# Feed-forward weights quantised and transposed inside the first group of time mixing, instead of in a stage of their own

## The chip, the cores and the metric

The kernel runs on one core of a Trainium2 chip. TensorE (PE), VectorE (DVE), ScalarE (ACT), GpSimd (POOL) and SyncE (SP) run side by side and wait for each other through semaphores. SyncE issues all the transfers of this program. The metric is the device time of one execution in microseconds; the time before is 2716.16 us, the median of three runs (2716.14 to 2721.93).

## The reference

One layer in three parts, each with a layer norm ahead and a residual behind: cross attention, time mixing (a recurrent state over 32 tokens) and a feed-forward with ternary weights. x is (128, 32, 256). The parts that the change touches:

```
x = x + xattn(layernorm(x), ctx)
x = x + time_mixing(layernorm(x))
x = x + ffn(layernorm(x))

def act_quant(x):                       # 8 bits per token
    scale = 127.0 / clip(max(abs(x), -1), EPS)
    return clip(round(x * scale), -128, 127) / scale

def weight_quant(w):                    # ternary
    scale = clip(mean(abs(w)), EPS)
    return clip(round(w / scale), -1, 1) * scale

def h_bitlinear(x, w):                  # fwht: Hadamard transform
    return act_quant(fwht(x)) @ weight_quant(w).T

gate, up = h_bitlinear(x, w_gate), h_bitlinear(x, w_up)     # (1024, 256) each
return h_bitlinear(silu(gate) * up, w_down)                 # (256, 1024)
```

## The kernel before

Cross attention runs first and ends at about 2010 us of the span. It leaves its result in DRAM. After a barrier `time_mixing` (line 1129) runs, then `feed_forward` (line 1688). Both are written out by hand: each engine has a list of its own, and semaphores join the lists.

**Time mixing** has the 128 sequences on the partitions and takes the 32 tokens in eight groups of T = 4. `run(step)` calls `step(j, j % 2)` for j = 0 to 9 on each engine. In step j, group j is mixed and projected, group j-1 goes through the recurrence (`scan_out`, `scan_in`, on VectorE with the state in PSUM), and group j-2 is normalised, gated, projected and stored. Group j+1 is transposed (`columns`, `shift`) and group j+2 normalised.

What group 0 goes through, in order:

- SyncE (lines 1213 to 1238): `load(0)` and `load(1)` bring two groups of rows; then fourteen loads of weights and small vectors, then 32 loads of eight values each (`gw` and `gb`, sixteen times each, lines 1224 to 1226), all on `w_loaded`; then `load(2)`, `load(3)`, and per group `load(j + 4)` and `store(j)`. A load of group j waits until group j-2 is normalised. `store(j)` loads the residual's rows into `xr`, waits for the result and stores `x2`.
- ScalarE (lines 1454 to 1462): sums, squares and normalisation of groups 0 and 1, the transposed columns of group 0, the tanh of `low_rank(0)`.
- VectorE (lines 1585 to 1594): waits for all of `w_loaded`, centres `wv` (two instructions, `vmean` and `wv`), then `shift(0)`: the difference `dT` and the first mixture `xp`.
- TensorE: `columns(0)`, waits for `w_loaded` and `wv_ready`, `low_rank(0)` (line 1260), then in `step` the mixes 0 to 3, `decay`, mixes 4 and 5, the transposes of group j-2, mixes 6 to 9 (each a product of 32 rows by 512 columns, line 1271), and the projections `project(j, 0..3)`, `low_rank(j + 1)` and `gates(j)`.
- Each mix goes from TensorE to VectorE (`mix`, line 1482) and to GpSimd (`xm`, line 1621). `decay` waits for the first two `xm`, `project(j, 0)` for the first eight.
- GpSimd also makes the layer norm's roots, the outer products `kv` and the column of the current token in `prod` (`own_values`, line 1640).

The tiles `x2`, `oT`, `o`, `sgT`, `osq` and `prod` are first written in the later steps: `prod` at `own_values(0)`, `sgT[0]` at `gates(0)`, `o[0]` and `osq` in step 1, `oT` and `x2` in step 2.

**The feed-forward** begins with a block of its own (lines 1707 to 1788): three weights of 1 MB are loaded, with the Hadamard matrix behind them. VectorE takes the absolute sum of each (line 1740), makes the scaled copies of the Hadamard matrix (lines 1744 and 1746), takes the scales from a product with a matrix of ones, and makes each weight ternary in three passes (lines 1757, 1759 and 1761: scale and min, max and add MAGIC, subtract MAGIC into bf16). TensorE transposes each in 16 pieces (line 1779) and ScalarE copies them to `wgT`, `wuT` and `wdT` (line 1788). The block ends with a barrier. Then the second block works through 32 tiles of 128 tokens (one per position), pipelined over six steps: it loads the rows `x`, transposes them (line 1868), copies them to `hT` (line 1966), rotates them with `had_x` (line 1898), quantises, and so on.

## Time and profile before

| what | value |
|---|---|
| median of three runs | 2716.16 us |
| lowest, highest | 2716.14, 2721.93 us |
| the profiled execution's own time | 2719.26 us |
| its span | 2717.5 us |
| mean granted TensorE clock | 0.939 |
| PE busy | 2492.1 us (92%) |
| DVE busy | 1983.9 us (73%) |
| ACT busy | 1666.3 us (61%) |
| POOL busy | 1203.6 us (44%) |

The page and the tables are of one execution, recorded by the hardware profiler. All positions in time are microseconds from the start of its span. A timeline row gives the start, the duration, the engine, the line, the operation, what it writes and reads, its shape and how many instructions are merged in the row; in brackets stands how long the engine was idle before, and what ended the wait. SPq rows are issues of transfers, not the transfers. The granted clock is a share of full speed: 1.00 is 2.4 GHz and 0.50 is 1.2 GHz.

### The profile page before, as it was taken

To read this page: it belongs to the slowest core of one execution; us is meant where nothing else is said; L and a number is where in the kernel's file an instruction comes from. 1 tells how busy PE (TensorE), PEld (TensorE's weight loads), DVE (VectorE), ACT (ScalarE), POOL (GpSimd) and SP (SyncE) were. 2 spreads that over 40 slices of the span, in tenths; PEclk is the share of its full clock that TensorE was granted. 3 is DMA by queue.
4 is the path that set the end of the run, shared out by engine and by line. 5 is a ranking of instruction groups with operands and counts; after the bars stand their busy time and mean duration, and the time that the engine had idled before them with its cause. 6 is when DMAs were issued, how large, how long until landed. Compare 5 with 4: busy or idle time off the path is not lost. (4 is left out here: it accounts for less than half of the span.)

```text
span 2717.5 us, 51029 instructions
## 1 busy us (share of the span) xinstructions
PE 2492.1 (92%) x14035; PEld 2025.8 (75%) x14035; DVE 1983.9 (73%) x4330; ACT 1666.3 (61%) x3281; POOL 1203.6 (44%) x1935
## 2 busy tenths in 40 slices
PE   8999999999979967999999999999959999838998
PEld 6777777777758857998989899899944454426886
DVE  7999999999956635776767676667734787867886
ACT  6777777777745535666666566666644444316776
POOL 2210111100137733655555555555626676606775
PEclk9999999999989988999999999999987787859999
DMA  3000000000012214344344333444420010021111
GB/s 120 24 26 26 26 26 26 26 26 26 20 45 67 66 30 153 114 115 112 113 118 118 112 117 110 114 113 116 116 87 16 24 47 16 32 71 43 53 52 39
DMA packets 234985, 183.49 MB, mean 68 GB/s; under 512 B 37169, under 2 KB 226834, under 8 KB 234258
## 3 DMA queue, kind: packets, MB, share of 16 engines
q1 hardware_dynamic: 234770, 180.90, 23.0%
q8 instruction: 101, 1.65, 0.3%
q14 instruction: 114, 0.93, 0.1%
HBM read 152.74 MB, written 28.06 MB: 67 GB/s over the span
## 5 line engine op out<-in xcount | busy, mean ns | idle before, releaser
L255 DVE TENSOR_REDUCE kn_ssq<-kn_sq 128x8 f32<-128x1024 f32 x514 | 621.2, 1215 | 72.4 <-ACT kn_sq L197 67.0
L197 ACT ACTIVATE kn_sq<-kn_keys 128x1024 f32<-128x1024 f32 x514 | 528.0, 1027 | 178.5 <-PE kn_keys L146 176.2
L146 PE MATMUL kn_keys<-kn_wk_hi,kn_ct_hi 128*128 128x512 f32 x1028 | 334.1, 406 | 0.9 <-ACT kn_sq L197 0.9
L146 PE MATMUL kn_keys<-kn_wk_lo,kn_ct_hi 128*128 128x512 f32 x1028 | 320.9, 393 | 0.0
L146 PE MATMUL kn_keys<-kn_wk_hi,kn_ct_lo 128*128 128x512 f32 x1028 | 320.4, 393 | 0.0
L1012 DVE CUSTOM_DVE_ANT_0 ca_sc<-ca_b_sc,ca_rk,ca_rq_rows 128x257 f32<-128x257 f32 x512 | 230.7, 482 | 82.2 <-issue 81.9
L967 ACT ACTIVATE ca_sc<-ca_sc,ca_low 128x257 f32<-128x257 f32 x512 | 254.4, 499 | 12.5 <-DVE ca_low L1045 4.8
L1115 POOL TENSOR_TENSOR ca_sc<-ca_sc,ca_rden 128x1028 f32<-128x1028 f32 x128 | 243.3, 1901 | 10.0
L146 PEld LDWEIGHTS kn_keys<-kn_wk_lo,kn_ct_hi 128*128 128x128 f32 x1028 | 193.3, 188 | 45.0
L146 PEld LDWEIGHTS kn_keys<-kn_wk_hi,kn_ct_lo 128*128 128x128 f32 x1028 | 193.3, 188 | 44.4
L146 PEld LDWEIGHTS kn_keys<-kn_wk_hi,kn_ct_hi 128*128 128x128 f32 x1028 | 165.3, 189 | 69.4 <-ACT kn_sq L197 55.9
L1113 POOL TENSOR_TENSOR ca_pl<-ca_sc,ca_rden 128x4 f32<-128x4 f32 x128 | 25.5, 199 | 418.0 <-DVE ca_rden L1067 418.0
L954 ACT ACTIVATE ca_pT_hi<-ca_b_p 128x512 fp32r<-128x512 f32 x256 | 139.7, 595 | 96.4 <-PE ca_b_p L869 96.4
L818 PE MATMUL ca_b_sc<-ca_cT_hi,ca_u_hi 128*128 128x258 f32 x512 | 161.5, 315 | 29.5 <-issue 10.6
L33 POOL TENSOR_TENSOR kn_mark<-kn_ident 1x1 f32<-1x1 f32 x66 | 12.1, 183 | 368.4 <-DVE kn_ssq L255 365.6
L1022 DVE TENSOR_TENSOR ca_oT_lo<-ca_b_val,ca_oT_hi 128x512 fp32r<-128x512 f32 x128 | 88.5, 692 | 110.7 <-ACT ca_oT_hi L974 110.7
L1050 DVE TENSOR_TENSOR ca_pT_lo<-ca_b_p,ca_pT_hi 128x512 fp32r<-128x512 f32 x256 | 164.9, 686 | 0.1
L818 PE MATMUL ca_b_out<-vo_hi,ca_oT_hi 128*128 128x256 f32 x512 | 155.4, 303 | 1.8 <-DVE ca_x L1035 1.8
L820 PE MATMUL ca_b_sc<-ca_cT_hi,ca_u_lo 128*128 128x258 f32 x512 | 147.5, 288 | 0.0
L819 PE MATMUL ca_b_sc<-ca_cT_lo,ca_u_hi 128*128 128x258 f32 x512 | 147.3, 288 | 0.0
L869 PE MATMUL ca_b_p<-ca_ident,ca_sc 128*128 128x128 f32 x1024 | 136.5, 276 | 9.4 <-issue 9.4
L819 PE MATMUL ca_b_out<-vo_lo,ca_oT_hi 128*128 128x256 f32 x512 | 144.4, 282 | 0.0
(316 smaller groups left out, 6770.9 us busy)
## 6 DMA issues: line engine op xcount, KB each, us to landing
ca_rk<-key_norms SPq DMA_DIRECT2D x512, 128.5 KB, 2.9
kn_rows<-in_ctx_dram SPq DMA_DIRECT2D x128, 128.0 KB, 2.4
ca_rows<-in_ctx_dram SPq DMA_DIRECT2D x128, 128.0 KB, 2.7
ca_xT<-normed_columns SPq DMA_DIRECT2D x16, 512.0 KB, 4.6
ca_vs_rows<-last_values SPq DMA_DIRECT2D x96, 64.0 KB, 2.6
qn_x<-in_x_dram SPq DMA_DIRECT2D x32, 128.0 KB, 2.5
normed_columns<-qn_xT_hi SPq DMA_DIRECT2D x32, 128.0 KB, 1.8
normed_columns<-qn_xT_lo SPq DMA_DIRECT2D x32, 128.0 KB, 1.8
```

The lines of the kernel that those rows point to most:

```text
L146: mm = pe.matmul(keys[c][:, n * 512:(n + 1) * 512], a, w[:, c * CH + n * 512:c * CH + (n + 1) * 512], start=first, stop=last)
L197: act.activation(sq[c][:, :], keys[c][:, :], ACT.Square).then_inc(sq_ready, 1)
L255: dve.tensor_reduce(ssq[s][:, t * H + c * (H // 2):t * H + (c + 1) * (H // 2)], sq[c][:, :].rearrange("p (h d) -> p h d", d=P), AX.X, ALU. ...
L818: pe.matmul(out, a_hi, w_hi, start=first, stop=False)
L819: pe.matmul(out, a_hi, w_lo, start=False, stop=False)
L820: return pe.matmul(out, a_lo, w_hi, start=False, stop=final)
L869: mm = pe.transpose(b_p[k][:, g * P:(g + 1) * P], s[:, g, k * P:(k + 1) * P], ident[:, :])
L954: act.activation(pT_hi[:, k, :], b_p[k][:, :], ACT.Copy).then_inc(phi_ready, 1)
L967: act.activation(sc[bb % 4][:, g, :], sc[bb % 4][:, g, :], ACT.Exp, bias=low[n][:, g:g + 1], scale=1.0, accum_out=den[n][:, g:g + 1]).then ...
L1012: dve.tensor_tensor_reduce(sc[bb % 4][:, g, :], b_sc[g % 2][:, 0:SKV], rk[n][:, g, :], rq_rows[i][:, bb % PER // 4, g, bb % 4:bb % 4 + 1], ...
L1050: dve.tensor_tensor(pT_lo[:, k, :], b_p[k][:, :], pT_hi[:, k, :].bitcast(F32), ALU.subtract).then_inc(plo_ready, 1)
L1115: pool.tensor_tensor(probs[:, :, :], probs[:, :, :], rden[m][:, :].unsqueeze(2).broadcast_to((P, 4, SKV)), ALU.mult)\
```

## The change

- The transposed weights (`ff_cols`) and their scales (`ff_scale`) are allocated outside both functions. `time_mixing` fills them and `feed_forward` gets them.
- The whole first block of `feed_forward` is gone, with its barrier. Its Hadamard load stands behind the first tile's load. Its scaled copies stand on VectorE between the statistics of tile 0 and of tile 1, and the rotation of tile 0 waits for them. The identity and the constants are made at the start of the remaining block.
- In `time_mixing` the raw weights are loaded in six halves of 512 KB, behind `wx1`, `wv`, `mu` and `load(1)` and ahead of the other weights. They lie in tiles that group 0 doesn't need yet (`x2`, `oT`, `o[1]`, `sgT[1]`, `osq`), and the ternary values in `prod`.
- VectorE takes six absolute sums ahead of its wait for `w_loaded`. The scales and the passes of weight 0 come after `shift(0)`, those of weight 1 after mix 3 of group 0, those of weight 2 after its mix 9. Each pass is two instructions of 1024 columns.
- TensorE transposes weight 0 between mix 3 and `decay(0)`, weight 1 between mix 5 and mix 6, weight 2 between `project(0, 1)` and `project(0, 2)`. ScalarE copies them out after `decay(0)`, after the squares of group 2, and after the last `take`. They use the PSUM banks `b_o`.
- The first uses of the borrowed tiles get waits: `scan_out` and `own_values` for the last transposes, `gates` and SyncE's first two row loads for the last ternary values.
- The 32 small loads stand behind `load(3)` on a semaphore of their own, `affine_loaded`, for which ScalarE waits at its first affine step.
- The residual's rows are loaded into `x2` itself. The load waits for the store of two groups before; `xr` is gone.

Time mixing's side, cut to its core:

```diff
+        raw = [w.rearrange("p a b -> p (a b)") for w in (x2[0][:, :, :], x2[1][:, :, :], oT[:, :, :], o[1][:, :, :], sgT[1][:, :, :])] + [osq[:, :]]
+        tern = [prod[n // 2][:, :, :, :].rearrange("p h v k -> p (h v k)").bitcast(BF16)[:, (n % 2) * F:(n % 2 + 1) * F] for n in range(6)]
...
-        WEIGHTS = 14 + 2 * (P // HV)
+        WEIGHTS = 14
...
             load(0)
+            sp.dma_start(wx1[:, :, :], wx1_dram.rearrange("(a p) n -> p a n", p=P)).then_inc(w_loaded, 16)
+            sp.dma_start(wv[:, :, :], wv_dram.rearrange("(a p) n -> p a n", p=P)).then_inc(w_loaded, 16)
+            for a in range(2):
+                sp.dma_start(mu[:, a:a + 1], mu_dram[a * P:(a + 1) * P].rearrange("(p a) -> p a", a=1)).then_inc(w_loaded, 16)
             load(1)
...
+            for n in range(2):
+                for h in range(2):
+                    sp.dma_start(raw[2 * n + h].rearrange("p (r n) -> p r n", r=4),
+                                 ff_dram[n].rearrange("(h r p) n -> h p r n", h=2, p=P)[h]).then_inc(raw_loaded[n], 16)
+            for h in range(2):
+                sp.dma_start(raw[4 + h], ff_dram[2][h * P:(h + 1) * P, :]).then_inc(raw_loaded[2], 16)
+            for w, d in ((wr, wr_dram), (wk, wk_dram), (wg, wg_dram), (ww1, ww1_dram), (wo, wo_dram)):
                 sp.dma_start(w[:, :, :], d.rearrange("(a p) n -> p a n", p=P)).then_inc(w_loaded, 16)
...
-            for a in range(2):
-                sp.dma_start(mu[:, a:a + 1], mu_dram[a * P:(a + 1) * P].rearrange("(p a) -> p a", a=1)).then_inc(w_loaded, 16)
...
-            for h in range(P // HV):
-                for w, d in ((gw, gw_dram), (gb, gb_dram)):
-                    sp.dma_start(w[h * HV:(h + 1) * HV, :], d.rearrange("(v a) -> v a", a=1)).then_inc(w_loaded, 16)
...
-                sp.dma_start(xr[n][:, :, :], x1_dram[:, T * j:T * (j + 1), :]).then_inc(xr_loaded[n], 16)
+
+                if j < 2:
+                    sp.wait_ge(ternary, 18)
+                ge(sp, x2_stored[n], 16 * (j // 2))
+                sp.dma_start(x2[n][:, :, :], x1_dram[:, T * j:T * (j + 1), :]).then_inc(xr_loaded[n], 16)
                 sp.wait_ge(x2_ready, 2 * (j + 1))
                 sp.dma_start(x2_dram[:, T * j:T * (j + 1), :], x2[n][:, :, :]).then_inc(x2_stored[n], 16)
             load(2)
             load(3)
+            for h in range(P // HV):
+                for w, d in ((gw, gw_dram), (gb, gb_dram)):
+                    sp.dma_start(w[h * HV:(h + 1) * HV, :], d.rearrange("(v a) -> v a", a=1)).then_inc(affine_loaded, 16)
             for j in range(GROUPS):
...
+            def weight_sums():
+                pe.wait_ge(ones_ready, 1)
+                pe.wait_ge(part_ready, 6)
+                for h in range(2):
+                    mm = pe.matmul(b_o[0][:, 0:3], ones[:, :], part[:, 3 * h:3 * h + 3], start=(h == 0), stop=(h == 1))
+                mm.then_inc(sum_filled, 1)
+
+            def turn_weight(n):
+                pe.wait_ge(identb_ready, 1)
+                pe.wait_ge(scale_ready, 2)
+                pe.wait_ge(ternary, 6 * (n + 1))
+                for a in range(2):
+                    ge(pe, cols_ready, 2 * (n - 1) + a + 1)
+                    out = b_o[a][:, :].bitcast(BF16)
+                    for r in range(8):
+                        half, col = (r // 4, (r % 4) * DIM + a * P) if n < 2 else (r % 2, (4 * a + r // 2) * P)
+                        mm = pe.transpose(out[:, r * P:(r + 1) * P], tern[2 * n + half][:, col:col + P], identb[:, :])
+                    mm.then_inc(w_turned, 1)
...
+                    if j == 0:
+                        turn_weight(0)
...
+                    if j == 0:
+                        turn_weight(1)
...
+                        if j == 0 and t == 1:
+                            turn_weight(2)
...
+            weight_sums()
             pe.wait_ge(w_loaded, 16 * WEIGHTS)
             pe.wait_ge(wv_ready, 2)
             low_rank(0)
...
+                act.wait_ge(ternary, 18)
...
+            def weight_columns(n):
+                for a in range(2):
+                    act.wait_ge(w_turned, 2 * n + a + 1)
+                    out = ff_cols[n][:, a, :] if n < 2 else ff_cols[n][:, 4 * a:4 * a + 4, :].rearrange("p c o -> p (c o)")
+                    act.activation(out, b_o[a][:, :].bitcast(BF16), ACT.Copy).then_inc(cols_ready, 1)
...
+                if j == 0:
+                    weight_columns(0)
...
+                if j == 0:
+                    weight_columns(1)
...
+                    act.wait_ge(affine_loaded, 32 * (P // HV))
...
+                    if j == 0:
+                        weight_columns(2)
...
+                    dve.wait_ge(w_turned, 6)
...
                     dve.tensor_tensor(x2[n][:, 2 * h:2 * h + 2, :].rearrange("p t d -> p (t d)"), b_o[h][:, :],
-                                      xr[n][:, 2 * h:2 * h + 2, :].rearrange("p t d -> p (t d)"), ALU.add).then_inc(x2_ready, 1)
+                                      x2[n][:, 2 * h:2 * h + 2, :].rearrange("p t d -> p (t d)"), ALU.add).then_inc(x2_ready, 1)
...
+            def weight_parts(n):
+                dve.wait_ge(raw_loaded[n], 32)
+                for h in range(2):
+                    dve.tensor_reduce(part[:, 3 * h + n:3 * h + n + 1], raw[2 * n + h], AX.X, ALU.add, apply_absolute_value=True).then_inc(part_ready, 1)
+
+            def weight_scales():
+                dve.wait_ge(sum_filled, 1)
+                dve.tensor_scalar(scale[:, :], b_o[0][:, 0:3], 1.0 / (F * DIM), EPS, ALU.mult, ALU.max).then_inc(scale_ready, 1)
+                dve.wait_ge(scale_ready, 1)
+                dve.reciprocal(inv[:, :], scale[:, :]).then_inc(inv_ready, 1)
+                dve.tensor_scalar(ff_scale[:, :], scale[:, :], 1.0 / 127.0, None, ALU.mult).then_inc(scale_ready, 1)
+
+            def weight_values(n):
+                dve.wait_ge(inv_ready, 1)
+                for k in (2 * n, 2 * n + 1):
+                    dve.tensor_scalar(raw[k], raw[k], inv[:, n:n + 1], 1.0, ALU.mult, ALU.min).then_inc(ternary, 1)
+                for k in (2 * n, 2 * n + 1):
+                    dve.wait_ge(ternary, 6 * n + 1 + k % 2)
+                    dve.tensor_scalar(raw[k], raw[k], -1.0, MAGIC, ALU.max, ALU.add).then_inc(ternary, 1)
+                for k in (2 * n, 2 * n + 1):
+                    dve.wait_ge(ternary, 6 * n + 3 + k % 2)
+                    dve.tensor_scalar(tern[k], raw[k], -MAGIC, None, ALU.add).then_inc(ternary, 1)
...
                 into(0)
+                if j == 0:
+                    weight_values(1)
                 mixes(4, 5, 6, 7, 8, 9)
+                if j == 0:
+                    weight_values(2)
...
+            for n in range(3):
+                weight_parts(n)
             dve.wait_ge(w_loaded, 16 * WEIGHTS)
...
             shift(0)
+            weight_scales()
+            weight_values(0)
             run(step)
...
+            pool.memset(ones[:, :], 1.0).then_inc(ones_ready, 1)
+            pool.wait_ge(ident_ready, 2)
+            pool.tensor_copy(identb[:, :], ident[:, :]).then_inc(identb_ready, 1)
...
+                pool.wait_ge(w_turned, 6)
```

The feed-forward's side; the deleted block stood ahead of the tiles of the first hunk:

```diff
-            for t in range(3):
+            load(0, 0)
+            sp.dma_start(had[:, :], had_dram).then_inc(had_loaded, 16)
+            for t in range(1, 3):
                 load(t, t)
...
+            pe.wait_ge(id_ready, 2)
             x_columns(0, 0)
+            pe.wait_ge(had_ready, 6)
             run(pe, step)
...
+            act.wait_ge(const_ready, 3)
...
+            dve.memset(mhalf[:, :], -0.5).then_inc(const_ready, 1)
+            dve.memset(magic[:, :], MAGIC).then_inc(const_ready, 1)
+            dve.memset(nmagic[:, :], -MAGIC).then_inc(const_ready, 1)
             statistics(0, 0)
+            dve.wait_ge(had_loaded, 16)
+            for k in range(4):
+                dve.tensor_scalar(had_x[:, k // 2, (k % 2) * P:(k % 2 + 1) * P], had[:, :], (-1.0 if k == 3 else 1.0) * DIM ** -0.5, None,
+                                  ALU.mult).then_inc(had_ready, 1)
+            dve.tensor_scalar(had_h[:, :], had[:, :], F ** -0.5, None, ALU.mult).then_inc(had_ready, 1)
+
+            dve.wait_ge(had_ready, 5)
+            dve.memset(had_x[:, :, 0:1], 0.0).then_inc(had_ready, 1)
             statistics(1, 1)
             run(dve, step)
...
+            make_identity(pool, ident, id_ready)
+            pool.wait_ge(const_ready, 1)
```

## Rows read from the trace of the kernel before

**Rows 1.** The page, section 1: busy time, share of the span, instructions.

```profile
PE 2492.1 (92%) x14035; PEld 2025.8 (75%) x14035; DVE 1983.9 (73%) x4330; ACT 1666.3 (61%) x3281; POOL 1203.6 (44%) x1935
```

**Rows 2.** Busy time by stage: stretch, length, engines, then granted clock, DMA, GB/s.

```profile
2247.00:2292.00 45.00, 41.51 (x128) 22.11 (x128) 32.69 (x41) 19.81 (x49) 29.78 (x31) 0.77 0.07 24
2292.00:2332.00 40.00, 37.12 (x129) 20.25 (x128) 33.35 (x40) 14.68 (x27) 28.02 (x27) 0.87 0.08 27
2415.00:2444.00 29.00, 6.23 (x50) 5.38 (x50) 19.05 (x24) 5.68 (x6) 0.93 (x4) 0.50 0.31 111
```

**Rows 3.** Timeline of SyncE's queue, end of mixing to first tile: start, us, issue.

```profile
2412.11 0.34 SPq L1232 DMA_DIRECT2D x_after_mixing<-tm_x  x1
2415.22 0.38 SPq L1721 DMA_DIRECT2D ff_w<-in_L_ffn_w_gate_dram  x1
...
2444.39 3.14 SPq L1845 DMA_DIRECT2D ff_x<-x_after_mixing  x5
```

**Rows 4.** Timeline of VectorE in the preamble: start, us, instruction, [idle before].

```profile
2426.42 2.29 DVE L1740 TENSOR_REDUCE ff_part<-ff_w 128x1 f32<-128x2048 f32 x1 [0.23 <-DMA ff_w<-in_L_ffn_w_down_dram]
2428.62 0.62 DVE L1744 TENSOR_SCALAR ff_had_x<-ff_had 128x128 f32<-128x128 f32 x4
...
2429.82 1.29 DVE L1757 TENSOR_SCALAR ff_w<-ff_w,ff_inv 128x2048 f32<-128x2048 f32 x1
...
2433.55 1.28 DVE L1757 TENSOR_SCALAR ff_w<-ff_w,ff_inv 128x2048 f32<-128x2048 f32 x1
```

**Rows 5.** Timeline of TensorE and of ScalarE, preamble and first tile.

```profile
2433.78 1.86 PE L1779 MATMUL ff_wbank<-ff_identb,ff_wt 128*128 128x128 bf16 x16 [4.43 <-DVE ff_wt L1761]
...
2447.65 2.07 PE L1898 MATMUL ff_b_y<-ff_had_x,ff_hT 128*128 128x256 f32 x4 [0.47 <-ACT ff_hT L1966]
...
2434.82 1.94 ACT L1788 ACTIVATE ff_wgT<-ff_wbank 128x1024 bf16<-128x1024 bf16 x2 [30.70 <-PE ff_wbank L1779]
...
2447.22 0.38 ACT L1966 ACTIVATE ff_hT<-ff_b_x 128x256 f32<-128x256 f32 x1 [3.08 <-PE ff_b_x L1868]
```

**Rows 6.** Timeline of VectorE, start of time mixing and group 0.

```profile
2031.35 0.69 DVE L1587 TENSOR_REDUCE tm_vmean<-tm_wv 128x64 f32<-128x512 f32 x1 [17.43 <-DMA tm_gb<-in_L_attn_gn_b_dram]
...
2042.53 0.69 DVE L1482 TENSOR_TENSOR tm_mix<-tm_b_t,tm_dT 128x512 f32<-128x512 f32 x1 [7.25 <-PE tm_b_t L1271]
...
2050.23 0.69 DVE L1482 TENSOR_TENSOR tm_mix<-tm_b_t,tm_dT 128x512 f32<-128x512 f32 x1 [4.25 <-PE tm_b_t L1271]
...
2062.32 1.50 DVE L1472 TENSOR_TENSOR tm_dT<-tm_xT,tm_b_t 128x512 f32<-128x512 f32 x2 [4.93 <-ACT tm_xT L1386]
```

**Rows 7.** Timeline of SyncE's queue, small loads and the loads behind.

```profile
2019.39 0.34 SPq L1226 DMA_DIRECT2D tm_gw<-in_L_attn_gn_w_dram  x1
...
2030.07 0.29 SPq L1226 DMA_DIRECT2D tm_gb<-in_L_attn_gn_b_dram  x1
2030.40 36.78 SPq L1212 DMA_DIRECT2D tm_xg<-x_after_attention  x3
```

**Rows 8.** Transfers from 2011 to 2040 us, rate in 40 slices of 0.725 us.

```profile
GB/s 0 0 107 260 429 384 381 345 360 353 323 323 241 46 21 0 0 0 0 0 0 0 11 0 0 0 0 0 147 305 271 0 0 96 220 379 28 0 0 0
```

**Rows 9.** Transfers from 2412 to 2450 us, rate in 40 slices of 0.95 us.

```profile
GB/s 4 405 142 0 84 199 363 369 305 382 373 428 425 382 80 0 0 0 0 0 0 0 0 0 0 0 0 0 0 0 0 0 0 0 0 181 279 109 130 8
```

**Rows 10.** Timeline of TensorE in group 0, the decay product.

```profile
2045.84 3.31 PE L1277 MATMUL tm_b_a<-tm_xm,tm_ww 128*64 128x512 f32 x4 [0.58 <-POOL tm_xm L1621]
```

**Rows 11.** Timeline of ScalarE in group 0.

```profile
2049.18 0.59 ACT L1401 ACTIVATE tm_hT<-tm_b_a 64x512 f32<-64x512 f32 x1 [6.27 <-PE tm_b_a L1277]
...
2059.13 0.38 ACT L1410 ACTIVATE tm_rk<-tm_b_a 128x256 f32<-128x256 f32 x1 [3.33 <-PE tm_b_a L1289]
...
2064.77 2.06 ACT L1377 ACTIVATE tm_xn<-tm_xg,tm_shiftn,tm_rstd 128x256 f32<-128x256 f32 x4
...
2072.18 0.60 ACT L1396 ACTIVATE tm_z<-tm_b_a 128x512 f32<-128x512 f32 x1 [2.20 <-PE tm_b_a L1260]
```

**Rows 12.** Timeline of GpSimd in group 0, additions that make xm.

```profile
2043.30 4.92 POOL L1621 TENSOR_TENSOR tm_xm<-tm_mix,tm_xT 128x512 f32<-128x512 f32 x4 [11.23 <-DVE tm_mix L1482]
```

111 lines of the change are left out of this document (21 added, 90 removed).

## The prediction

> **What bounds the kernel now.** I read the page first, to see that no engine fills the whole span [rows 1], then a table by stage. The stretch from 2415 to 2444 us stands out: TensorE does 6.2 us of work in 29, VectorE 19.1 [rows 2]. It is the feed-forward's preamble, alone between two barriers. SyncE's queue gives its ends: the last store of the mixed rows is issued at 2412.11, the first weight load at 2415.22, and the first feed-forward tile only at 2444.39 [rows 3]. Inside it one chain runs: loads of 1 MB, three absolute sums on VectorE, three passes over each weight, transposes, copies [rows 4, 5]. Nothing of the time mixing or of the tiles runs beside it. The second place is the start of time mixing. VectorE sits idle 17.4 us until the last tiny load (`gb`) lands, at 2031.35 [rows 6]. SyncE issues 32 of those, from 2019.39 to 2030.4, about 0.34 us each [rows 7]. Everything from there to 2078 is a serial fill of group 0, in which TensorE is the busiest engine.
>
> **Part 1: the preamble goes.** With it go the 29.17 us from 2415.22 to 2444.39 [rows 3]: loads, sums, ternary passes, transposes, copies and one barrier. The first tile's load now stands where the first weight load stood. Term: -29.2.
>
> **Part 2: the Hadamard matrix at the head of the tiles.** It was prepared under the preamble. Now its load is second in the queue (0.4 us after the first tile's), and VectorE makes the scaled copies after the first statistics: four in 0.62 us [rows 4], so one more is about 0.2, then a wait and a memset of 0.1. Before, the tile's wait ended at about 2446.5, the columns were copied at 2447.22 and the first rotation began at 2447.65 [rows 5], 1.2 us after the landing. The new chain is: matrix landed 0.4 us after the tile, 0.9 us of copies, 0.1 memset, some 0.2 of semaphores, so 1.6 to 1.7 us. Term: +0.5 (bounds 0, if statistics and landing overlap better, and +1.5). The constants and the identity are made before the tile lands: nothing. `statistics(1)` follows in VectorE's idle time.
>
> **Part 3: when time mixing can start.** Moved past the wait are 32 tiny issues (11 us of queue); put ahead of it are 3.15 MB of weights. So the limit turns from issues to bytes. Before, 2.59 MB moved at 107 and 260, then around 362 GB/s [rows 8]; the three weights alone moved at 305 to 428, mean about 378 [rows 9]. After, 5.74 MB: 0.27 MB by 2013.9, the other 5.47 MB at 370 GB/s takes 14.8 us, so 2028.7, and 0.5 to be seen: 2029.2. At 428 GB/s it is 2027.2, at 305 it is 2032.3. The last raw weight is 4.62 MB into the queue and so there at 2026.2. Its two half sums cost as much as the one of 2.29 us did [rows 4] plus 0.1, and end at 2028.6; the sums are hidden just, and the scale matmul with them. So VectorE's wait ends at 2029.2 instead of 2031.3: -2.1 (bounds -4.0 and +1.0). Nothing else holds it: group 0's normed columns were ready at 2025.9, and ScalarE's work on group 1 only has to be there by 2060. The tiny loads now lie between `load(3)`, which can go at 2034, and `load(4)`, which went only at about 2066.8 [rows 7] since it waits for group 2's normalisation; 11 us of issues fit in between. They are wanted at group 0's affine step, about 2130.
>
> **Part 4: the weights' work inside group 0.** VectorE: scales 0.5, then per weight three passes. One full weight took 3.73 us from pass one to the next weight's [rows 4]; in halves it is six instructions of about 0.65, 3.9 (bounds 3.7 and 4.2).
> - Weight 0 lies after `shift(0)`, while TensorE does the low-rank product and ScalarE the tanh. VectorE idled 7.25 us there [rows 6]; 4.4 go in. Nothing. The cover gone, it would be 4.4.
> - Weight 1 lies after mix 3, at 2045.98 by the old clock times. VectorE idled 4.25 us until mix 4 at 2050.23 [rows 6]; 3.9 go in. Nothing.
> - Weight 2 lies after mix 9 and before `shift(1)`, where it idled 4.93 us until 2062.32 [rows 6]; 3.9 go in. Nothing.
>
> TensorE: 16 bf16 transposes took 1.86 us at the 1.2 GHz level [rows 5]; the faster level is not seen for them, I take half, 0.95, as its bound.
> - Turn 0 goes ahead of the decay product. TensorE idled 0.58 us there for GpSimd's `xm` [rows 10], so the path gets 1.86 - 0.58 = 1.3 at the low clock, 0.4 at the high one. The clock is between the levels there. I take 0.9.
> - Turn 1 goes between mixes 5 and 6, at about 2051 + 0.9. It also waits for ScalarE's two copies of turn 0 (1.94 us for both [rows 5]), which follow the tanh of the decay, done at 2049.8 + 0.9 [rows 11], so the second half can start at about 2052.6 and the whole ends 1.0 to 1.9 us after mix 5. Mixes 6 to 9 and `project(0)` come later by that; GpSimd's `xm` 7 and 8 had some 0.4 us to spare. I take 1.3.
> - Turn 2 goes between `project(0, 1)` and `project(0, 2)` at the high clock. ScalarE normalises group 2 there for 2.06 us [rows 11], so most of the 0.95 is hidden: +0.4 (0 to 1.0).
>
> ScalarE: copies of turn 1 lie after group 2's squares, copies of turn 2 before the tanh of group 1, in holes of 3.3 and 2.2 us [rows 11]: nothing, as both are 1.94. Queued behind the new waits are: on GpSimd `own_values` and on VectorE `scan_out`, both on the sixth turn (about 2068), wanted at 2071 and 2080. SyncE waits for all ternary values (2063) ahead of the row load of `store(0)`, which it only reached at 2067. Sum of part 4: +2.6 (bounds +1.4 and +4.5).
>
> **Part 5: residual in the result's tile.** The same two additions of 0.69 each. The row load waits for the store of two groups ago, issued over 60 us earlier. Nothing; exposed, it would be a load of 3.5 us in each of eight groups.
>
> **Sum.** -29.2 + 0.5 - 2.1 + 2.6 = -28.2. Against the profiled execution's own 2719.26 us (span 2717.5, and 1.8 around it) this gives 2691.1. The median of the runs is 2716.16, 3.1 lower; I carry the difference over: 2688.0.
>
> **Two readings that could move it.** TensorE's granted clock changes inside every group. A group of 45 us had 0.77 of full speed, the next, of 40 us and nearly the same instructions, 0.87 [rows 2]. So 5 us hang on how the stretches fall. I put the clock term at 0, with 5 either way.
> The other is VectorE beside GpSimd. In group 0 GpSimd's four `xm` additions run unbroken for 4.92 us from 2043.30 [rows 12], and no VectorE instruction with only SBUF operands runs beside them. The trace of before has the ternary passes only where GpSimd is idle, so it neither shows nor excludes that they hold each other up. The Trainium skill (page "SBUF — State Buffer", section "Who interferes with whom") says that a VectorE `tensor_scalar` in its two-port mode and a GpSimd instruction exclude each other for a whole instruction. No run here shows it yet.
>
> **Rivals.**
> - *The passes and GpSimd take turns.* The price comes from rows: weight 1 meets two `xm` additions of 1.25 us [rows 12], so it ends 2.5 us later, 2052.4 against 2051.1 for mix 4: +1.3. Weight 2 meets two more, and ends at 2063.8 against 2062.3: +1.5. Together 2690.8, and up to 2697 if `normalise(2)` is pushed too. For it: both use SBUF only. Against: the holes are nearly as wide as the work. It is the rule cited above, worked out in this kernel.
> - *The start doesn't get earlier* (the change doesn't do that part of what it says): the 3.15 MB take the place of the issues, at 305 GB/s or less. +3.1 on the sum, so 2691 to 2694. For it: slices of 305 and 323 in the rates. Against: the mean is above 360 in both stretches.
> - *Kinder start or clock.* Bytes at 428 GB/s (-1.9) and five microseconds of clock: 2681.
> - *A part of the preamble stays exposed*, say one wait in a circle of new semaphores that holds group 0 by 12 us or more: 2700 to 2724.
> - *Slower than before: the clock.* If the new start puts TensorE out of step so that all eight groups sit longer at the low level, each 0.1 of mean clock costs 5 us a group [rows 2]. To reach 2724.3 it has to eat 28.2 + 8.1 = 36.3 us, 4.5 in each of eight groups. From there on the change loses; at 0.13 less in each group, it would be 6.5 x 8 = 52, so 2740. For it: the clock already moves from group to group. Against: seven of the eight groups keep their instructions.
>
> **How the numbers follow.** Forecast 0.50 (own range 2683 to 2693), taking turns 0.20, start not earlier 0.12, kinder 0.10, partly exposed 0.05, slower 0.03. The range from 2679 to 2699 leaves out the last two and the tails of kinder and of taking turns, some 0.15 in all. A difference within 0.3% (8.1 us) can't be told from none here. Faster 0.94, same 0.03 (part of the partly exposed case), slower 0.03.
>
> **What would show it.** In the trace of after: the first tile's load about 3 us after the last store; the first rotation 1.6 to 1.7 us behind its landing; VectorE's `vmean` at about 2029.2; six blocks of eight transposes in group 0, each ternary pass about 0.65 us and mix 4 not late; GpSimd's `xm` still at 1.25. It is wrong if `vmean` waits for a raw weight's sum beyond 2032, if a ternary pass is much longer than 0.65 beside GpSimd, or if the groups after the first change their lengths.

## The result, and the profile after

The changed kernel takes 2693.18 us (median of four runs, 2691.06 to 2693.76); the kernel before took 2719.05 us beside it (four runs, 2716.14 to 2722.61). The ratio is 0.9903, with a 95% interval of 0.9886 to 0.9920. The change makes the kernel faster by 25.9 us. The profiled execution took 2692.93 us, with a span of 2691.1 us against 2717.5.

The page of the changed kernel, section 1, has the columns of [rows 1]:

```profile
PE 2486.5 (92%) x14037; PEld 2022.7 (75%) x14037; DVE 1986.4 (74%) x4342; ACT 1665.8 (62%) x3281; POOL 1207.9 (45%) x1935
```

The engines have as much to do as before: VectorE is busy 2.5 us longer, GpSimd 4.3, ScalarE the same within 0.5, and TensorE has two instructions more (it is busy 5.6 us less, at a mean granted clock of 0.945 instead of 0.939). What went is a stretch in which they waited for each other.

I compare the two traces by landmarks that both have, so that each stretch has its own difference:

| stretch | before, us | after, us | difference | predicted |
|---|---|---|---|---|
| start of the span to mixing's first load | 2011.59 | 2010.54 | -1.1 | 0 |
| first load to VectorE's `vmean` | 19.76 | 19.62 | -0.1 | -2.1 |
| `vmean` to mix 0 of group 0 | 11.18 | 12.24 | +1.1 | 0 |
| mix 0 to mix 4 of group 0 | 7.70 | 9.04 | +1.3 | +0.9 |
| mix 4 to mix 9 | 6.47 | 7.67 | +1.2 | +1.3 |
| mix 9 to mixing's last store | 355.41 | 354.08 | -1.3 | +0.4 |
| last store to the tiles' first load | 32.28 | 3.09 | -29.2 | -29.2 |
| tiles' first load to the end | 273.11 | 274.82 | +1.7 | +0.5 |
| sum | 2717.5 | 2691.1 | -26.4 | -28.2 |

The first row is code that the change doesn't touch; other runs of the same changed kernel had 2008.37 and 2008.65 there. It is scatter, about as large as the terms below, and the reason why the experiments are read from landmarks. Each landmark is of one execution, though, and inside group 0 they scatter too: in seven traces that have this group 0 unchanged (the changed kernel and the later kernels that change other parts alone), mix 0 of group 1 comes 66.98 to 70.63 us after the first load, mostly by TensorE's clock.

SyncE's queue in the changed kernel, from the end of mixing, answers to [rows 3]:

```profile
2413.19 0.34 SPq L1252 DMA_DIRECT2D x_after_mixing<-tm_x  x1
2416.28 0.33 SPq L1855 DMA_DIRECT2D ff_x<-x_after_mixing  x1
2416.66 0.43 SPq L1867 DMA_DIRECT2D ff_had<-in_hadamard_dram  x1
```

The tile's load stands 3.09 us after the last store. Before, the first weight's load stood there, 3.11 us after it, and 29.17 us lay between that and the tile's load.

The same queue at the start of mixing answers to [rows 7], and below it is VectorE's `vmean` (its bracket is the idle time before it and what ended that):

```profile
2010.54 0.34 SPq L1223 DMA_DIRECT2D tm_xg<-x_after_attention  x1
...
2015.56 2.30 SPq L1235 DMA_DIRECT2D tm_sgT<-in_L_ffn_w_down_dram  x1
...
2021.12 1.79 SPq L1237 DMA_DIRECT2D tm_wo<-in_L_attn_Wo_dram  x1
...
2025.00 0.37 SPq L1242 DMA_DIRECT2D tm_bonus<-in_L_attn_bonus_dram  x1
2025.41 8.69 SPq L1223 DMA_DIRECT2D tm_xg<-x_after_attention  x2
...
2030.16 0.69 DVE L1680 TENSOR_REDUCE tm_vmean<-tm_wv 128x64 f32<-128x512 f32 x1 [1.53 <-DMA tm_bonus<-in_L_attn_bonus_dram]
```

The last load that `vmean` waits for is issued at 2025.00 instead of 2030.07, five microseconds sooner. It lands no sooner, counted from the first load, since 5.74 MB have to go through. With them goes `load(2)`, issued at 2025.41. The rates in 40 slices of 0.725 us, from 2010 to 2039, stand against [rows 8]:

```profile
GB/s 0 0 107 282 382 364 346 362 268 274 374 362 370 367 350 350 373 373 414 402 355 335 319 317 340 326 287 220 28 0 0 0 0 0 141 271 311 0 0 0
```

Group 0 on VectorE, weight 1's three passes in two halves each (here counted as six) and the mixes around them; this is the place of [rows 6]:

```profile
2042.40 0.69 DVE L1546 TENSOR_TENSOR tm_mix<-tm_b_t,tm_dT 128x512 f32<-128x512 f32 x1 [4.18 <-PE tm_b_t L1294]
...
2045.77 1.67 DVE L1617 TENSOR_SCALAR tm_oT<-tm_oT,tm_inv 128x1024 f32<-128x1024 f32 x1
2047.36 1.75 DVE L1617 TENSOR_SCALAR tm_o<-tm_o,tm_inv 128x1024 f32<-128x1024 f32 x1
2049.03 0.68 DVE L1620 TENSOR_SCALAR tm_oT<-tm_oT 128x1024 f32<-128x1024 f32 x1
...
2050.84 0.68 DVE L1623 TENSOR_SCALAR tm_prod<-tm_o 128x1024 bf16<-128x1024 f32 x1
2051.44 1.27 DVE L1546 TENSOR_TENSOR tm_mix<-tm_b_t,tm_dT 128x512 f32<-128x512 f32 x2
```

TensorE and GpSimd in the same stretch, against [rows 10, 12]:

```profile
2034.23 6.34 PE L1283 MATMUL tm_b_a<-tm_xp,tm_wx 128*128 128x512 f32 x8 [4.47 <-DVE tm_xp L1540]
...
2045.06 1.07 PE L1347 MATMUL tm_b_o<-tm_identb,tm_prod 128*128 128x128 bf16 x16
2046.06 1.93 PE L1300 MATMUL tm_b_a<-tm_xm,tm_ww 128*64 128x512 f32 x4
2047.92 1.98 PE L1294 MATMUL tm_b_t<-tm_z,tm_wx 32*128 32x512 f32 x4
2051.78 1.05 PE L1347 MATMUL tm_b_o<-tm_identb,tm_prod 128*128 128x128 bf16 x16 [1.88 <-DVE tm_prod L1623]
...
2043.17 5.39 POOL L1719 TENSOR_TENSOR tm_xm<-tm_mix,tm_xT 128x512 f32<-128x512 f32 x4 [11.54 <-DVE tm_mix L1546]
...
2062.26 1.71 POOL L1710 TENSOR_TENSOR tm_rstd<-tm_varx,tm_mhalf 128x4 f32<-128x4 f32 x1
```

Weight 1's first two passes take 1.67 and 1.75 us while GpSimd's `xm` run (2043.17 to 2048.56). From 2049.03 on, with GpSimd idle, each takes 0.68. The bracket of turn 1 shows who pays: TensorE waits 1.88 us for the ternary values. Mix 4 follows the last pass without a gap, although TensorE had the products of mixes 4 and 5 done by 2049.9.

### The profile page after: what moved, and what is told of

The parts are those of the page before. It is cut to its first block and busy times, and to the rows that moved or that the text cites. A ratio compares the mean times of both kernels' runs of the same rounds, so it can differ in the third digit from the quotient of the medians.

```text
span 2691.1 us, 51061 instructions
## 1 busy us (share of the span) xinstructions
PE 2486.5 (92%) x14037; PEld 2022.7 (75%) x14037; DVE 1986.4 (74%) x4342; ACT 1665.8 (62%) x3281; POOL 1207.9 (45%) x1935
## 5 line engine op out<-in xcount | busy, mean ns | idle before, releaser
L148 PEld LDWEIGHTS kn_keys<-kn_wk_lo,kn_ct_hi 128*128 128x128 f32 x1028 | 193.5, 188 | 45.6
L299 POOL TENSOR_TENSOR kn_step<-kn_ms,kn_rough 128x128 f32<-128x128 f32 (+1 forms) x33 | 15.1, 458 | 290.5 <-DVE kn_rough L264 290.4
```

Of the source, the lines that this page charges most:

```text
L148: mm = pe.matmul(keys[c][:, n * 512:(n + 1) * 512], a, w[:, c * CH + n * 512:c * CH + (n + 1) * 512], start=first, stop=last)
```

## The experiments

### The whole turned into two: the small loads

The change moves the small loads and puts 3.15 MB in front. Two kernels take these two parts one at a time. The first is the kernel before with the small loads moved and nothing else:

```diff
-        WEIGHTS = 14 + 2 * (P // HV)
+        WEIGHTS = 14
...  (before)
-            for h in range(P // HV): ... .then_inc(w_loaded, 16)
...  (behind load(3))
+            for h in range(P // HV): ... .then_inc(affine_loaded, 16)
...
+                    act.wait_ge(affine_loaded, 32 * (P // HV))
```

> The kernel before with one part of the change alone: the 32 small loads stand behind load(3) on their own semaphore; nothing else. Theory (the wait at the start of time mixing was the queue's issues, and the change only refills it with bytes): the fourteen other loads are there 9 us after the first, VectorE's shift(0) then waits for the group's own columns (14.3 us after the first load), the low-rank product starts at about 17.1 us after the first load instead of 23.8, and the kernel is 6 to 7 us faster than before (ratio 0.9975). Rival (the wait has another cause, as the 17.4 us of VectorE are put down to the last load only because it is the last): low rank starts less than 3 us earlier, and the time is within 3 us of before.

It took 2709.08 us (seven runs) against 2716.26 (ten runs), a ratio of 0.9973 (0.9962 to 0.9984): 7.2 us for moving 32 tiny issues.

The second is the changed kernel with that move taken back.

> The changed kernel with the 32 small loads back in their old place, ahead of load(2) and on the common semaphore. The last of the other loads is issued 14.5 us after the first and has landed at 19.6. Theory (bytes set the start, issues would set it later): 32 issues of 0.34 us end at 25.7 us after the first, vmean starts at about 26.4 instead of 19.6, and the kernel is 6 to 7 us slower than the changed one (about 2699.5, ratio to before 0.993). Rival (the start is set by the absolute sums and not by the landing): vmean would move by less than 2 us.

It took 2698.34 us against the same 2716.26, 0.9933 (0.9916 to 0.9949). The changed kernel itself wasn't timed beside it; the nearest to it there, the one with the residual's own tile (further down), took 2691.52, so 6.8 us less. VectorE's `vmean` in both, first the small loads moved alone, then moved back:

```profile
2019.78 0.69 DVE L1588 TENSOR_REDUCE tm_vmean<-tm_wv 128x64 f32<-128x512 f32 x1 [8.28 <-DMA tm_bonus<-in_L_attn_bonus_dram]
```

```profile
2035.36 0.69 DVE L1679 TENSOR_REDUCE tm_vmean<-tm_wv 128x64 f32<-128x512 f32 x1 [8.70 <-DMA tm_gb<-in_L_attn_gn_b_dram]
```

From the first load (2009.17 and 2008.34) these are 10.61 and 27.02 us, against 19.76 before and 19.62 after. Moving the small loads gives 9.1 us at `vmean`, of which 7.1 are left at the low-rank product (16.69 against 23.83), since the normed columns of group 0 are late next. In the changed kernel `vmean` is at 19.62 again: the raw weights ahead of the others take all of it back.

### The raw weights behind mixing's own loads

If so, the six raw halves should go behind mixing's weights. Their sums then come after `shift(0)`, and the three weights' passes and turns each one hole later: weight 2's passes at the end of step 0, its turn in step 1. The ternary values get tiles of their own.

```diff
-            for n in range(2):      # raw halves, ahead of wr, wk, wg, ww1, wo
-                for h in range(2):
-                    sp.dma_start(raw[2 * n + h]..., ff_dram[n]...).then_inc(raw_loaded[n], 16)
...  (behind bonus, ahead of load(2))
+            for n in range(2):
+                for h in range(2):
+                    sp.dma_start(raw[2 * n + h]..., ff_dram[n]...).then_inc(raw_loaded[n], 16)
...
-                    weight_values(1)
+                    weight_scales()
+                    weight_values(0)
...
-                    weight_values(2)
+                    weight_values(1)
...
+                if j == 0:
+                    weight_values(2)
```

> The changed kernel with the 3 MB of raw weights behind all loads that time mixing needs, and the weights' work one hole later: absolute sums after shift(0), weight 0 after mix 3, weight 1 after mix 9, weight 2 at the end of step 0; transposes after mix 5, after project(0, 1), and in step 1; the ternary values in tiles of their own. Theory (the change gives the gain of the moved small loads away by putting bytes ahead of them): vmean at 10.6 us after the first load as with the small loads alone, the low-rank product at 16.7 instead of 23.7, mix 0 at 25 to 25.5, mix 0 of group 1 at 65 to 66 instead of 69.8, and the kernel 4 to 7 us shorter than the changed one (ratio 0.988 to 0.989). Rival (the weights' work doesn't fit the later holes, and VectorE becomes the bound of group 0): low rank as early, but mix 0 of group 1 not before 69, and the time within 1 us of the changed kernel.

Beside it ran the changed kernel again:

> The changed kernel as it is, timed again, so that the next two are compared with it on one chip. All theories: 25 to 27 us faster than before (ratio 0.9903 to 0.991), and the same places in the trace: vmean 19.6 us after the first load, mix 0 of group 1 69.8 us after it, the feed-forward's tiles 274.8 us.

The new order took 2687.09 us (2682.80 to 2692.99), 0.9886 (0.9866 to 0.9905); the changed kernel 2691.12 us (2690.81 to 2692.19), 0.9897 (0.9881 to 0.9914); the kernel before 2719.52 us. `vmean` came 11.99 us after the first load, the low-rank product 16.80, and mixing's last store 396.42, against 402.86 in the changed kernel's own second trace. Mix 0 of group 1 came at 64.32, against 70.14, so the rival (not before 69) falls. The 6.4 us are there in the trace, and 4.0 in the medians; but the runs scatter by 10 us here and the intervals overlap, so the times alone don't show the gain. With the next kernel it has the lowest median of the study, 32 us under the kernel before.

`vmean` was expected at 10.6, as with the small loads moved alone, and came 1.4 later. The same fourteen loads stand ahead of it in both. There the next load was issued at 11.82 us after the first, behind `vmean`; here the raw weights follow at once, from 7.81 on. Bytes that `vmean` doesn't wait for, issued behind those that it does, seem to hold it up. No run tests this by itself.

The trace also has the strongest case of VectorE and GpSimd holding each other up. Weight 2's passes lie beside the outer products `kv`:

```profile
2067.91 2.43 DVE L1620 TENSOR_SCALAR tm_sgT<-tm_sgT 128x1024 f32<-128x1024 f32 x1
...
2067.37 2.43 POOL L1727 TENSOR_TENSOR tm_kv<-tm_rk,tm_v 128x1024 f32<-128x1024 f32 x1
```

The pass takes 0.68 alone, and `kv` 1.95 in the same trace where no pass is beside it. Together each takes 2.43.

### Passes where GpSimd rests

In the changed kernel GpSimd is idle for 11.5 us ahead of its first `xm`. So weight 1's passes go right behind weight 0's, where nothing shares with them:

```diff
             weight_values(0)
+            weight_values(1)
...
-                if j == 0:
-                    weight_values(1)
                 mixes(4, 5, 6, 7, 8, 9)
```

> The changed kernel with one edit: the three passes of weight 1 stand right behind those of weight 0, in VectorE's idle time before mix 0 (4.2 us), where GpSimd has nothing to do. In the changed kernel they take 5.67 us (2045.77 to 2051.44) where weight 0's take 3.8, and mix 4 starts 1.66 us after its cover was used up. Theory (VectorE's passes and GpSimd's additions take turns): weight 1's passes now take 3.8 to 3.9 us, with no instruction above 0.75 us; GpSimd's first four xm are back at 4.92 us; mix 4 starts 2.0 to 2.4 us earlier against mix 0, TensorE's wait of 1.88 us ahead of turn 1 is gone, and the kernel is 1 to 2.4 us shorter. Rival (the passes of halves that were loaded to other tiles are slow by themselves, or the wait is for TensorE): the passes stay at 5.7 us wherever they stand, mix 0 comes 1.5 us later, and the time is the same or longer.

It took 2687.18 us (2685.50 to 2691.45) against 2716.26, 0.9894 (0.9878 to 0.9911). The durations went as expected: six passes in 3.82 us, `xm` at 1.26, and no wait of TensorE ahead of turn 1. The gain in mix 4 did not show: it came 42.45 us after the first load, against 40.90. In that run TensorE's clock was lower in group 0 already ahead of the moved passes: 6.80 us for the low-rank product and 5.52 for mixes 0 to 3, against 6.34 and 3.88 (and the profiled execution was the slowest of its four). So this trace can't be set against that of the changed kernel above. I ran it again with the changed kernel beside it.

> The changed kernel with weight 1's passes right behind weight 0's, as once before, now beside a fresh copy of the changed kernel on the same chip. Theory (the turn-taking costs time): TensorE's wait of 1.9 us for the ternary values and the 1.8 us by which the passes are stretched go, so the medians differ by 1 to 3 us, this one lower, and group 0 ends 1 to 2 us sooner after the first load. Rival (it only moves the wait: the clock in group 0 or GpSimd's own xm additions are what is late next): medians within 1 us of each other, and the first mix of group 1 no sooner.

> The changed kernel once more, as the measure for the run beside it. Both theories: span 2689 to 2692, the first mix of group 1 at 69.8 to 70.2 us after mixing's first load, weight 1's passes 5.7 us for six, vmean at 19.5 to 19.8.

Now both have the same start (low-rank product 6.24 us at 23.98 us, mix 0 at 32.05 and 32.04). The medians are 2688.28 us (2687.56 to 2689.32) and 2690.83 us (2688.95 to 2691.80), the kernel before 2718.11; 0.9888 (0.9870 to 0.9906) and 0.9895 (0.9878 to 0.9913). The timelines with the passes moved, VectorE, TensorE and GpSimd:

```profile
2036.87 0.75 DVE L1617 TENSOR_SCALAR tm_oT<-tm_oT,tm_inv 128x1024 f32<-128x1024 f32 x1
...
2040.00 0.69 DVE L1623 TENSOR_SCALAR tm_prod<-tm_o 128x1024 bf16<-128x1024 f32 x1
...
2047.70 0.69 DVE L1546 TENSOR_TENSOR tm_mix<-tm_b_t,tm_dT 128x512 f32<-128x512 f32 x1 [3.22 <-PE tm_b_t L1294]
...
2048.46 1.28 PE L1347 MATMUL tm_b_o<-tm_identb,tm_prod 128*128 128x128 bf16 x16
...
2041.80 4.93 POOL L1718 TENSOR_TENSOR tm_xm<-tm_mix,tm_xT 128x512 f32<-128x512 f32 x4 [12.04 <-DVE tm_mix L1546]
```

| after the first load, us | before | changed, beside it | passes moved |
|---|---|---|---|
| mix 4 | 38.64 | 41.08 | 38.72 |
| mix 9 | 45.11 | 48.86 | 44.61 |
| first mix of group 1 | 67.04 | 70.04 | 66.19 |
| mixing's last store | 400.52 | 402.73 | 399.23 |

Moving six passes to 7 us earlier brings mix 4 forward by 2.36 us, to where it was without any weights' work. What the turns cost there, the faster clock gave back. Between mix 4 and mix 9 another 1.89 us go. The windows of 4 us show why (length, busy time of PE, PEld, DVE, ACT and POOL with counts, then the granted clock, DMA share, GB/s); first the changed kernel, then the one with moved passes:

```profile
2046.00:2050.00 4.00, 2.12 (x8) 0.83 (x9) 4.00 (x6) 2.41 (x3) 0.57 (x1) 1.00 0.00 0
2050.00:2054.00 4.00, 4.00 (x21) 2.12 (x18) 1.42 (x3) 1.07 (x5) 3.24 (x4) 0.63 0.00 0
```

```profile
2046.00:2050.00 4.00, 3.96 (x23) 1.85 (x22) 1.38 (x2) 2.41 (x3) 2.26 (x3) 1.00 0.00 0
2050.00:2054.00 4.00, 3.55 (x8) 0.95 (x6) 2.49 (x4) 2.81 (x9) 3.56 (x4) 1.00 0.00 0
```

TensorE is busy 2.12 of 4 us while it waits for the passes, and then its clock falls to 0.63, and to 0.50 in the next 4 us (1.00 is 2.4 GHz, 0.50 is 1.2). With the passes moved it is busy 3.96, and stays at 1.00 for four more microseconds. So in this pair, which has one clock up to mix 3, the turn-taking costs time, and its rival, that the wait only moves, falls: group 1 starts 3.85 us sooner, not at the same time. Later groups take some of it back. The sum `tm_var` of group 0, two steps further on, is 5.06 us sooner, and mixing's last store 3.50. The lengths between the eight `tm_var` sums were 45.5 41.3 42.8 45.6 40.2 38.9 25.6 in the changed kernel and 42.7 45.5 41.3 42.8 44.5 39.1 25.6 with moved passes, 1.5 us more in all. 2.55 us remain in the medians, with ranges that overlap by 0.4 us.

How much the passes cost hangs on the clock. The changed kernel's second trace (the one beside the raw weights moved behind) has the slower clock in group 0, like the first trace with the passes moved. These two belong side by side. First the changed kernel, then the passes moved:

```profile
2039.41 5.68 PE L1294 MATMUL tm_b_t<-tm_z,tm_wx 32*128 32x512 f32 x8 [0.68 <-ACT tm_zl L1446]
...
2045.73 0.74 DVE L1617 TENSOR_SCALAR tm_oT<-tm_oT,tm_inv 128x1024 f32<-128x1024 f32 x1
2046.39 1.75 DVE L1617 TENSOR_SCALAR tm_o<-tm_o,tm_inv 128x1024 f32<-128x1024 f32 x1
...
2050.48 1.50 DVE L1546 TENSOR_TENSOR tm_mix<-tm_b_t,tm_dT 128x512 f32<-128x512 f32 x2
```

```profile
2039.54 5.52 PE L1294 MATMUL tm_b_t<-tm_z,tm_wx 32*128 32x512 f32 x8 [0.68 <-ACT tm_zl L1446]
...
2050.64 0.69 DVE L1546 TENSOR_TENSOR tm_mix<-tm_b_t,tm_dT 128x512 f32<-128x512 f32 x1 [4.84 <-PE tm_b_t L1294]
```

There one pass is stretched instead of two, TensorE doesn't wait ahead of turn 1, and mix 4 comes 9.91 us after mix 0, against 9.94 with the passes moved: moving them gains nothing. At the faster clock the same distance is 9.04 and 6.67. So the 2.36 us at mix 4 are the price where the clock is at 1.00 through mixes 0 to 3.

### The residual from a tile of its own

```diff
+        xr = [sb(f"xr{n}", [P, T, DIM]) for n in range(2)]
...
-                ge(sp, x2_stored[n], 16 * (j // 2))
-                sp.dma_start(x2[n][:, :, :], x1_dram...).then_inc(xr_loaded[n], 16)
+                sp.dma_start(xr[n][:, :, :], x1_dram...).then_inc(xr_loaded[n], 16)
...
+                ge(dve, x2_stored[n], 16 * (j // 2))
```

> The changed kernel with the residual's rows loaded into a tile of their own again. Theory (that part is worth nothing, since the store it waits for is over 60 us old): within 1 us of the changed kernel, ratio 0.9903 to 0.991, and each group's additions start as before. Rival (the row load's new wait or its later start costs in the last groups): 1 to 3 us faster than the changed kernel, with earlier row loads in SyncE's timeline.

2691.52 us (2688.53 to 2693.53), 0.9915 (0.9898 to 0.9931). Mixing's last store came 400.50 us after the first load here, 2.2 sooner than after; but the passes are stretched the same and the groups behind group 0 have the same lengths. The first difference is in group 0 (mix 0 at 30.96 against 31.86), ahead of any residual. TensorE waited only 0.30 us ahead of turn 1 in this trace. No effect of the residual's tile can be told from scatter.

### The head of the tiles

The tiles took 274.82 us from their first load, 1.7 longer than before. The head in the changed kernel, VectorE and TensorE (against [rows 5]):

```profile
2419.00 0.60 DVE L2080 TENSOR_SCALAR ff_had_x<-ff_had 128x128 f32<-128x128 f32 x4
...
2419.92 2.08 PE L1910 MATMUL ff_b_y<-ff_had_x,ff_hT 128*128 128x256 f32 x4 [0.71 <-DVE ff_had_x L2085]
```

The first rotation begins 3.64 us after the tile's load, against 3.26 before: 0.38 us of the 1.7. The rest follows TensorE's clock. Windows counted from the first tile's load, 12 to 14, 14 to 16, 16 to 24 and 24 to 26 us behind it; before, then after:

```profile
2456.39:2458.39 2.00, 2.00 (x6) 0.76 (x4) 1.45 (x7) 1.11 (x2) 0.00 (x0) 0.53 0.00 0
2458.39:2460.39 2.00, 1.22 (x6) 0.43 (x6) 1.97 (x4) 1.16 (x4) 0.00 (x0) 1.00 0.36 103
2460.39:2468.39 8.00, 5.48 (x29) 3.26 (x28) 5.37 (x17) 3.86 (x8) 7.29 (x11) 1.00 0.13 40
2468.39:2470.39 2.00, 1.60 (x9) 0.79 (x7) 1.34 (x7) 1.32 (x3) 1.95 (x2) 1.00 0.00 0
```

```profile
2428.28:2430.28 2.00, 1.51 (x8) 0.62 (x5) 1.43 (x7) 1.06 (x2) 0.00 (x0) 0.92 0.00 0
2430.28:2432.28 2.00, 1.19 (x5) 0.43 (x6) 1.97 (x4) 1.05 (x4) 0.00 (x0) 1.00 0.45 131
2432.28:2440.28 8.00, 5.47 (x25) 3.37 (x24) 5.30 (x17) 3.63 (x7) 7.36 (x11) 0.91 0.11 33
2440.28:2442.28 2.00, 2.00 (x8) 1.44 (x7) 0.00 (x0) 0.83 (x2) 1.92 (x3) 0.51 0.00 0
```

The clock rises about 1 us sooner than before and, 22 to 26 us behind the load, falls back for some 3 us, which it did not do before. One kernel tests whether the Hadamard matrix at the head is the reason: it is loaded and scaled in step 1 of mixing.

```diff
+                if j == 1:       # VectorE, in time_mixing
+                    dve.wait_ge(had_loaded, 16)
+                    for k in range(4):
+                        dve.tensor_scalar(had_x..., had[:, :], ...).then_inc(had_ready, 1)
...
-            pe.wait_ge(had_ready, 6)
-            dve.wait_ge(had_loaded, 16)
```

> The changed kernel with the Hadamard matrix loaded behind the small loads and its scaled copies made in step 1 of time mixing. The tiles took 273.1 us with the preamble and 274.8 without; 0.4 of the 1.7 is the later first rotation, and the rest a stretch of TensorE at 0.5 to 0.6 of full clock 22 to 26 us after the first tile's load, which is in all four traces without preamble and in neither with it. Theory A (the stretch comes from the later rotation, which shifts the tiles against the clock): rotation 3.25 us after the load, no such stretch, tiles 273.1 us, the kernel 1.7 us shorter. Theory B (the stretch comes from what TensorE did before the tiles, which the preamble changed): rotation 3.25 us after the load, the stretch stays, tiles 274.2 to 274.5, the kernel 0.4 us shorter.

2694.10 us (2692.15 to 2694.99), 0.9909 (0.9892 to 0.9925), beside 2691.12 for the changed kernel. The rotation came 3.38 us after the load, 0.26 sooner, the clock fell back all the same (0.91, then 0.51), and the tiles took 275.95 us. So the matrix at the head is not the reason for the fall, and moving it away gains nothing, where both theories had it 0.4 to 1.7 us shorter. Why its tiles are 1.1 us longer I can't say.

Two kernels move the tiles against what went before, by three and six tiny loads (waited for) ahead of the first tile:

```diff
+            for k in range(3):      # six in the second kernel
+                sp.dma_start(pad[8 * k:8 * k + 8, :], had_dram[8 * k:8 * k + 8, 0:8]).then_inc(pad_loaded, 16)
+            sp.wait_ge(pad_loaded, 16 * 3)
```

> The changed kernel with three loads of 256 bytes ahead of the first tile's load, which goes about 1.0 us later. In four kernels without preamble (also the one whose first rotation is 0.26 us earlier) the granted clock rises at the same distance from the last store, and falls to 0.5 to 0.6 for some 3 us at 22 to 26 us after the first tile's load; with preamble it doesn't. Theory (the instants at which the clock can change are set by what went before and don't follow the tiles): the rise comes 1 us sooner after the load, and the low stretch moves or goes; tiles measured from the load shorter than 274.8 us, by up to 1.7. Rival (the clock follows the tiles' own work): rise and low stretch stay at 12.2 and 22 to 26 us after the load, tiles 274.8.

> The same with six such loads, so that the first tile's load goes about 2.0 us later. Theory (clock's instants set by what went before): the rise comes 2 us sooner after the load than in the changed kernel, and the low stretch at 22 to 26 us is gone or elsewhere. Rival (the clock follows the tiles' own work): the same clock rows as in the changed kernel, counted from the load, and tiles of 274.8 us.

Each was run once, with 2721.56 us for the kernel before: 2692.04 and 2695.92 us. Single times say nothing of a microsecond, so I read the traces alone, and they too are one of each. The load came 4.10 and 5.11 us after the last store instead of 3.09. With three, the clock rose between 15 and 16 us after the last store, as in the changed kernel, so 1 us sooner counted from the tiles; the fall stayed; the tiles took 274.67 us. With six, it rose between 18 and 19 us after the last store and there was no fall, as before the change (windows 12 to 14 and 16 to 24 us behind the tile's load):

```profile
2430.49:2432.49 2.00, 2.00 (x8) 0.82 (x6) 1.26 (x6) 0.60 (x2) 0.00 (x0) 0.58 0.00 0
...
2434.49:2442.49 8.00, 5.47 (x28) 3.10 (x28) 5.70 (x18) 3.80 (x7) 6.98 (x11) 1.00 0.14 45
```

Yet its tiles took 275.61 us, 0.8 more than with the fall. So in these traces the fall comes and goes with how far the tiles stand behind the work ahead of them, and it isn't what makes the tiles 1.3 us longer, or not alone. That rest stays open.

## Why the prediction was right, and where not

The time, 2693.18 us, lies inside the range of 2679 to 2699 and 5.2 us above the forecast. The forecast difference was 28.2 us; measured were 25.9, and 27.3 and 28.4 beside the two later copies. The prediction carried over a median of 2716.16 for the kernel before, which measured 2719.05 beside this result: 2.9 of the 5.2 are that. The traces, 2717.5 and 2691.1 us, differ by 26.4, 1.8 less than forecast. The measured time is 0.2 us beyond the main reading's own range (2683 to 2693), and two of its rivals turned out to be at work.

- **Part 1, the preamble, -29.2: right**, to 0.02 us (29.17 between the loads, and 3.09 against 3.11 ahead of them).
- **Part 2, the Hadamard matrix, +0.5: right** as a term (+0.38). Missed was that the tiles' later course moves as well, by 1.3 us. The prediction's clock term of 0 with 5 either way covered it without naming the tiles.
- **Part 3, the start of mixing, -2.1: mis-sized; it was -0.1.** The prediction let 5.47 MB go at 370 GB/s in 14.8 us. The 23 full slices of the rates above have a mean of 348, which makes 15.7 us (+0.9). And `load(2)`, which `vmean` doesn't wait for, is issued at 2025.41 and moves in the last of these slices. By the rates 6.1 MB had moved at 2029.7, half a microsecond ahead of `vmean`, and only 5.74 MB of them stand ahead of `load(2)`: some 0.37 MB were its own, about 1.0 us at the same rate. That this is what held `vmean` up is worked out, not tested. The prediction did not count it. The absolute sums are not the cause: VectorE sat idle 1.53 us between the last of them and `vmean`. The rival "the start doesn't get earlier", given 0.12, is the one that came true here. Its price of +3.1 was for 305 GB/s; it was +2.0. The prediction also costed the 32 issues at the old place and never asked what they cost alone: that was 9.1 us at `vmean`, of which 7.1 were left at the low-rank product, without the raw weights in front.
- **Part 4, group 0, +2.6: the size was near, the items were wrong.** From mix 0 to mix 9 it was +2.5. The prediction gave the passes nothing and the turns 0.9, 1.3 and 0.4. The runs show the reverse. TensorE was at 1.00 there up to turn 1: turn 0 took 1.07 us and the decay product behind it 1.93, against 3.31 in [rows 10], so that the decay product was done sooner than before. With the passes moved away, mix 4 came at 38.72 us, against 38.64 before the change, though mix 0 came 1.1 later: between the two the turn cost less than the clock gave. In that pair the passes cost 2.4 at mix 4, and 1.9 more by mix 9 through the clock; at the slower clock they cost nothing at mix 4. The rival "the passes and GpSimd take turns", given 0.20, is what happens: its price for mix 4 was +1.3, and it was +2.4 at the faster clock. The step that failed is "3.9 go in. Nothing": weight 1's passes took 5.7 us and weight 2's 4.8. The first two passes of weight 1 alone are 2.1 longer than 0.65 each. The prediction had named this as a sign of being wrong ("if a ternary pass is much longer than 0.65 beside GpSimd"), and it came true, although the time lay inside the range. What turns 1 and 2 cost by themselves no run shows.
- **The rule of the Trainium skill** (page "SBUF — State Buffer", section "Who interferes with whom") agrees with these traces: passes at 0.68 alone and at 1.67, 1.75 and 2.43 beside GpSimd, and GpSimd's `rstd` at 1.71 against 1.04 elsewhere. The same section says that a VectorE instruction with two SBUF inputs contends with a GpSimd instruction that reads SBUF. The trace agrees: GpSimd's `shiftn` took 0.72 us beside VectorE's centring of `wv` (below), and 0.20 for the group before.

```profile
2030.88 0.69 DVE L1682 SCALAR_TENSOR_TENSOR tm_wv<-tm_vmean,tm_wv 128x512 f32<-128x512 f32 x1
...
2030.91 0.72 POOL L1712 TENSOR_TENSOR tm_shiftn<-tm_nmean,tm_rstd 128x4 f32<-128x4 f32 x1
```

- **Part 5, the residual, 0: right**, as far as runs with 2 us of scatter can tell.
- **The clock over the later groups, 0: right.** The two windows of [rows 2], at the same place in the changed kernel:

```profile
2247.00:2292.00 45.00, 41.24 (x128) 21.96 (x127) 33.38 (x40) 19.94 (x49) 29.79 (x31) 0.77 0.07 24
2292.00:2332.00 40.00, 37.09 (x129) 20.18 (x128) 33.39 (x40) 14.58 (x27) 28.06 (x27) 0.87 0.08 27
```

The clocks are 0.77 and 0.87 again, so the rival of eight slower groups never began. Group 0 did lose 1.1 us to the clock between `vmean` and mix 0: the low-rank product took 6.34 us, against 5.27, and the granted clock some 3 to 6 us behind its start was 0.59 (2037 to 2040), against 0.93 before (2038 to 2041). Mixing as a whole, from its first load to its last store, took 2.1 us longer than before.

The total came nearer than the parts, and that is luck. Against the forecast, 2.0 were lost in part 3, 1.1 to the clock of the low-rank product and 1.2 in the tiles; 1.1 of scatter ahead of mixing and 1.7 behind mix 9, which the prediction doesn't have and no run explains, made up for most of it.

## What to carry to other kernels

When a wait is bound by issues, price the reordering alone before filling the queue's free time with other bytes: 32 tiny loads moved behind gave 7.2 us, and in the traces 3.15 MB put in front took it back. Put what the next instruction needs first in the queue, and the work for later behind it: the first instruction that waited came 7.5 us sooner, though the medians, 4.0 us apart, scatter too much to prove the gain. Before calling a hole in VectorE's timeline free for a pass over SBUF, look at what GpSimd does in it: here a hole beside GpSimd stretched the pass from 0.68 to as much as 2.43 us. Moving six passes to a hole common to both gave 2.36 us at the next mix where TensorE's clock was high, nothing where it was low, and 2.55 us in the medians. And take the changed kernel's trace more than once: one pair of traces alone would have said 2.4 us, another nothing.
